# Start-up loads gathered on SyncE's queue, and the next group's first up-projection weights issued ahead of a down-projection

## The reference

```python
# attention half
g = layernorm(x) @ Wg.T + bg ;  v = layernorm(x) @ Wv.T + bv
corr = cosine(g_i, g_j) on the window j in [i-128, i], else 0; corr = (corr+1)/2
denom = mean_j(corr) + 0.5 ; fit = 1 / (denom * sum_i(1/denom))
attn = softmax over the window of corr * fit
x = x + (attn @ v) @ Wo.T + bo
# feed-forward half
h = square(relu(layernorm(x) @ W_fc.T))      # 2048 x 4096
y = h @ W_proj.T                             # 2048 x 1024
mem = 0; five times: mem = 0.9*mem + y - (mem > 1); count += (mem > 1)
out = x + count / 5
```

## Time and profile before

| | us |
|---|---|
| median of 2 runs, slowest core | 1675.33 (1674.3 to 1676.35) |
| the profiled execution, slowest core | 1668.64 |
| its span from first to last instruction, core 0 | 1666.8 |
| spans of the other cores | 1651.3 to 1664.4 |
| TensorE busy, core 0 | 1016.7 (61%) |
| VectorE busy | 690.2 (41%) |
| ScalarE busy | 668.2 (40%) |
| mean granted TensorE clock, by core | 0.783 to 0.788 |

### The profile page before, as it was taken

How to read it: one execution, slowest core, us unless ns; L and a number is a source line. 1 busy time by engine, 2 the same in 40 slices (tenths; PEclk the granted TensorE clock), 3 DMA queues, 4 the chain that set the end, 5 groups by cost and what they waited for, 6 DMA issues and landing times.

```text
span 1666.8 us, 16466 instructions; the slowest of 8 cores (1651.3 to 1666.8 us)
## 1 busy us (share of the span) xinstructions
PE 1016.7 (61%) x4568; PEld 432.6 (26%) x4632; DVE 690.2 (41%) x1639; ACT 668.2 (40%) x1467; POOL 131.1 (8%) x216
## 2 busy tenths in 40 slices
PE   0013555578566656666656887886788868878800
PEld 0012222233222222222222333332333323333300
DVE  1300222210655655565543011099207950494098
ACT  1245323233466666666664552153304530341000
POOL 1011221111000000000000100110011101111100
PEclk9999777789555555555557999999899979999955
DMA  9977665454000000000004444443544444445311
GB/s 189 219 155 163 101 101 106 112 118 108 1 1 1 1 1 1 1 1 1 1 1 139 115 138 138 128 132 120 190 126 127 152 163 128 126 152 169 108 31 45
DMA packets 78908, 158.69 MB, mean 95 GB/s; under 512 B 38627, under 2 KB 38884, under 8 KB 78820
## 3 DMA queue, kind: packets, MB, share of 16 engines
q0 software_dynamic: 63824, 106.97, 26.9%
q1 hardware_dynamic: 12608, 46.14, 8.2%
q10 hardware_dynamic: 2388, 4.54, 0.9%
HBM read 147.15 MB, written 33.55 MB: 108 GB/s over the span
## 4 chain that ended last, share of the span: by engine, by line
DMA 30%; PE 24%; DVE 20%; issue 11%; ACT 10%; another core or an unknown queue 3%; POOL 1%; DVEq 1%; ACTq 0%; POOLq 0%; SPq 0%
PE psY L834 8%; DMA wpb<-wprojC 7%; DMA wstg<-wfcT 7%; DMA wstg<-wprojT 5%; PE psY L796 4%; ACT ebf L526 4%; DMA wfcb<-wfcC 4%; ACT PT L585 4%; DVE memb L873 4%; DMA wfcC<-wstg 4%; DVE t1b L870 3%; DMA wprojC<-wstg 3%; PE psPV L599 3%; DVE accb L881 3%
## 5 line engine op out<-in xcount | busy, mean ns | idle before, releaser
L796 PE MATMUL psY<-x2nT,wfcb 128*128 128x512 bf16 x1003 | 231.8, 385 | 51.3 <-DMA wfcb<-wfcC 48.6
L834 PE MATMUL psY<-wpb,h_sb 128*128 128x512 bf16 x1002 | 233.9, 388 | 40.1 <-DMA wpb<-wprojC 38.0
L599 PE MATMUL psPV<-PT,v_sb 128*64 128x128 bf16 x512 | 104.2, 307 | 99.2 <-ACT PT L585 99.2
L526 ACT ACTIVATE ebf<-C,fit 128x256 f32<-128x256 f32 x256 | 151.4, 591 | 2.3 <-DVE em L565 0.6
L796 PEld LDWEIGHTS psY<-x2nT,wfcb 128*128 128x128 bf16 x1024 | 98.4, 99 | 184.0 <-issue 77.4
L834 PEld LDWEIGHTS psY<-wpb,h_sb 128*128 128x128 bf16 x1024 | 98.9, 100 | 174.0 <-issue 71.3
L577 PE MATMUL psPT<-ident_sb,em 128*128 128x128 bf16 x512 | 98.0, 295 | 56.3 <-DVE em L565 56.3
L862 DVE TENSOR_SCALAR spkA<-y 128x1024 f32<-128x1024 f32 x16 | 11.1, 694 | 273.8 <-ACT y L852 272.5
L852 ACT ACTIVATE y<-psY 128x512 f32<-128x512 f32 x32 | 16.1, 625 | 264.2 <-PE psY L834 264.2
L805 ACT ACTIVATE frb<-psY 128x512 f32<-128x512 f32 x128 | 76.6, 599 | 111.3 <-PE psY L796 111.2
L565 DVE SCALAR_TENSOR_TENSOR em<-ebf,rqb,maskA_sb 128x256 bf16<-128x256 f32 x240 | 112.9, 473 | 0.5 <-issue 0.5
(11 more groups left out here) (99 smaller groups left out, 1225.1 us busy)
## 6 DMA issues: line engine op xcount, KB each, us to landing
wfcb<-wfcC POOLq DMA_DIRECT2D x64, 512.0 KB, 4.1
wpb<-wprojC POOLq DMA_DIRECT2D x64, 512.0 KB, 3.9
xa<-xin SPq DMA_DIRECT2D x32, 512.0 KB, 4.9
wstg<-wfcT POOLq DMA_DIRECT2D x32, 256.0 KB, 5.6
wfcC<-wstg POOLq DMA_DIRECT2D x16, 512.0 KB, 3.0
wstg<-wprojT POOLq DMA_DIRECT2D x16, 512.0 KB, 5.2
wprojC<-wstg POOLq DMA_DIRECT2D x16, 512.0 KB, 2.9
x2d<-x2t SPq DMA_DIRECT2D x16, 512.0 KB, 2.9
```

The source lines that it names most:

```text
L526: e = b.op("S", lambda h, hb=hb, qt=qt, q4=q4: h.activation(ebf[q4][:], C_sb[hb][:, 256 * qt:256 * qt + 256], AF.Exp, scale=fitb[hb][:, qt ...
L599: mpv = b.op("T", lambda h, h_i=h_i, hp=hp, qt=qt, q4=q4, pb=pb, half=half: h.matmul(psPV[pb][hp:hp + 64, 128 * (q4 % 2):128 * (q4 % 2) + ...
L796: mmt = b.op("T", lambda h, f=f, fp=fp, k=k, gi=gi: h.matmul(psY[f % 2][:], wfcb[fp % 2][:, 1024 * (f % 2) + 128 * k:1024 * (f % 2) + 128 ...
L834: last = b.op("T", lambda h, f=f, f2=f2, tti=tti, nh=nh, pj=pj: h.matmul(psY[pj][:], h_sb[:, 512 * f + 128 * tti:512 * f + 128 * tti + 128 ...
```

## The change

Three edits. The eleven constants are issued on SyncE's queue in place of ScalarE's. All eight x pairs are issued on SyncE's queue. And the first two `wfcb` loads of the next group's up-projection are issued at the beginning of `emit_proj_scan(gi)` for gi = 0, 1, 2, ahead of all `wpb` loads of that down-projection, where they stood behind them; `emit_fc` takes them from a dictionary. No transfer is added or removed, and no buffer either.

```diff
-        tok_pre = b.dma("S", "pre", dst[:], src[:])
+        tok_pre = b.dma("Y", "pre", dst[:], src[:])
...
-        qeng = "Y" if j == 0 else "S"
+        qeng = "Y"
...
+    fc_pre = {}
...
+    def fc_preload(gi):
+        fc_pre[gi] = [b.dma("G", f"wfs{i}", wfcb[i][:],
+                            wfcC[:, 2048 * i:2048 * (i + 1)],
+                            waits=[wfcb_free[i], tok_wcache])
+                      for i in range(2)]
+
     def emit_fc(gi):
-        tok_wf = [None, None]
+        tok_wf = fc_pre.pop(gi, [None, None])
         for f in range(NF):
             pf = f % 2
             fp = f // 2
-            if f % 2 == 0:
+            if f % 2 == 0 and (tok_wf[fp % 2] is None or fp >= 2):
                 tok_wf[fp % 2] = b.dma("G", f"wfs{fp % 2}", wfcb[fp % 2][:],
...
     def emit_proj_scan(gi):
         nonlocal scan_free, h_free
+        if gi + 1 < 4:
+            fc_preload(gi + 1)
         while pend_outs:
```

## The result

The changed kernel took 1681.69 us in the median of 43 runs (1671.15 to 1705.24); the kernel before, with more runs, 1676.49 in the median of 42 (1666.34 to 1697.54). The ratio of the two is 1.0035 with a 95% interval of 1.0019 to 1.0051: the change costs about a third of a per cent, 6 us. Ratios leave out the executions in which a die ran slower at a lower granted clock; the only profile of part 2 alone is of such an execution, and its landmarks are not used. The forecast was 2 us less than before. The measured time lies inside the forecast range, but the direction is wrong.

A forecast was written before the change was run, and what follows sets the result against it. The weight cache's chain was taken to set the attention start, with slack in stage A. 1668.64 + 0 (queues) - 2 (earlier up-projection loads) = 1666.6 us profiled; as a median 1675.33 - 2, about 1673, range 1661 to 1683.

The forecast's parts named there:

- What bounds the kernel: Whole timeline: the cache's last write sets the attention start, stage A has slack; a core's time is that start plus 1251 us.
- Part 1, the head: Constants and x pairs on SyncE's queue: stage A's first transpose at 82 instead of 95.9 us, worth nothing at the attention.
- Part 1, the chain: Weight cache's first write: one more x pair ahead (6 MB, not 5) delays it 3.2 us, from 65.45 to 68.7.
- Part 1, the next round: Cache's first round: 3 MB beside it, not 4, so 20.2 us, ending at 88.9 as before; sum taken 0.
- slower, because the weights are pushed back: Rival at the cache's chain: chain and attention start move by 9.6 us, time about 1683; chance 0.15.
- the likeliest case: Whole kernel: the forecast of about 1673, together with "nothing at all" (1675); chance 0.67, range 1668 to 1678.
- Its mark of 73 us or later: Sign of the slower rival, at the cache's chain: first wfcC write comes at 73 us or later.
- its second mark: Sign of the slower rival, at the cache's chain: the round following the first write still above 20 us.
- Both rivals on the faster side: Cache's chain gets ahead: 1660, chance 0.15; or stage A's earlier start counts: 1659, chance 0.03.
- the signs named beforehand: Trace after: attention's first matmul at 412 to 419, then 1251 us; refuted if cache's last write moves 10 us or more.
- Part 2: Feed-forward half, first two up-projection loads ahead: no wait removed, down-projections sooner; -2 us taken, bounds -3.8 to +1.6.

The follow-up runs named there:

- part 2 alone: Only the first two up-projection loads issued ahead of the down-projection, start as in the kernel before; ratio to that kernel 0.9989 (0.9959 to 1.0018).

## Why the prediction was wrong

**What bounds the kernel: right.** The attention's start set by the cache's chain, with slack in stage A on all cores, is what the run without that wait shows. That a core's time is its attention start plus 1251 was read too sharply: the means over eight cores of span minus start lie between 1252.0 and 1256.8 in nine kernels that have the old feed-forward order, and at 1255.8, 1254.1 and 1254.4 in three with the new. The profile before was at the low end, and its own cores go from 1248.5 to 1254.9; core 5 of the changed kernel had 1260.1. So no cost of part 2 can be read from that sum.

**Part 1, the head: right in kind, too hopeful in size.** 82 us was forecast for stage A's first transpose on core 0, 86.3 came (9.6 us won, not 14), and the mean of the cores won only 6.5, since core 0 was one of the late ones before. The sum of turns was right for six pairs: forecast to land at 28.5, 35, 43, 49, 57 and 63, they are used on core 0 at 30.1, 36.0, 44.2, 50.8, 58.6 and 64.6. The last two came 4 to 5 us late, at 73.2 and 79.9, where 69 and 75 had been taken "with the weights gone". The weights and the first wstg load were not gone. That these us are worth nothing at the attention was right.

**Part 1, the chain: this step failed.** "So pair 5, which moves ahead of the chain's first write (6 MB there, where 5 were), holds the weights back by 3.2 us". It was 9 MB, where 5 were, and 15.5 us. The price per MB holds roughly (3.5 us for the first one more, 3.9 over all four); the amount was counted against the old end of the weights, 65.45 us, though each MB that gets in moves that end and lets more in. At 4 MB and 3.2 us this makes 12.8 us, and the constants' move adds 1.0. Of the 15.5, 1.7 us remain that no run settles; the stretched tail of the small packets is the place where they would be.

**Part 1, the next round: half right.** It was to give back all that the first write lost. The round was to shrink from 23.5 to 20.2 us on core 0 and make up for the 3.2; in the mean it shrank from 21.6 to 16.2 us, more than forecast, for only 1.2 MB of x was left to travel beside it, but against a delay of 15.5. Then nothing is left to give back but 2.3 us over the remaining 30 rounds: those are a chain of waits. The rival "slower, because the weights are pushed back" had the mechanism, and 9.6 us for it; 7.8 came in the attention's start and about 6 in the time. That the time still fell into the forecast's range is owed to that rival, into which the range reached, and not to the likeliest case. Its mark of 73 us or later for the first write was met on all cores; its second mark, a round above 20 us, was not. It had been given 0.15. Both rivals on the faster side fell: no core had its first write before 77 us, and no core started its attention by stage A.

Of the signs named beforehand, the cache's last write moved by 7.8 us in the mean, less than the 10 that would have refuted the forecast, and still the forecast failed; the sign was too wide. The attention's first matmul came at 422.0 on the latest core, outside 412 to 419. The stretch from there to the end was off 1251 by more than 5 us on four cores, but since kernels with the old order show the same spread, that says nothing against part 2.

**The Trainium skill's rule.** The round robin between queue rows ("DMA: Bandwidth & Descriptors", Queues, rings and completion order) was used for x against 2 KB weight packets, where the turns cost the same. It says more than I drew from it: if the turns are near one for one, a stream of small packets suffers most beside one of large packets. The trace bears this out in direction: 475 small against 342 large packets in 70 to 75 us, where the same load alone had 1763 in 5 us. It doesn't show turns one for one: in 65 to 70 it was 1208 to 209, and in 75 to 80 it was 321 to 172. The page also counts several descriptors to a packet, and whether the packets of these traces are such is not shown.

**Part 2: right in kind.** No DMA wait at fc's first matmul to remove; the down-projections shorter by 0.5, 1.1 and 1.2 us, where up to 1.2 was allowed for the first two and less for the third; b2 before proj(0) longer by 1.7, where up to 1.6 was allowed and nothing taken, and b2 before proj(2) by 1.3. Together about 0, where -2 was forecast, and 0.9989 (0.9959 to 1.0018) measured, from which neither can be told.

## What to carry to other kernels

Before making a stream of loads earlier, write down what shares the DMA engines with it and which of the two has slack: here x had 5 to 18 us and the weight cache none, and the change took from the second to give to the first. Count what gets in against the moved end of the other stream, not the old one. And look at who needs what first: ordering the loads by first use, and taking from a stage's entry the waits that it doesn't need, was worth 3.1%, some nine times what the moved queues cost.

## What the runs showed of the hardware

A load in packets of 256 bytes, which needed 5 us with the engines to itself (1763 packets in 5 us), took about 15 us beside a stream of 4 KB packets on another queue (342 + 1208 + 475 + 321 packets in 20 us, the first stretch with the end of the weights in it; the load has 2048). I had priced it by its bytes, with the same cost per MB as the large packets.

The attention ran next to undisturbed beside the cache's rounds: from the attention's start to the first b2 matmul it took 464.7 and 464.3 us with the cache's wait removed, against 464.3 and 463.9 with it. With the loads held, where the cache travels beside the attention's first 96 us, it took 464.6 and 464.2.
